# Roots on GpSimd instead of a Newton chain, and a later turn of the normalised row, in a sequence of 48 rows

## The reference

```python
def l2norm(t):
    return t / jnp.maximum(jnp.linalg.norm(t, axis=-1, keepdims=True), 1e-12)

def attn_layer(x, Wqkv, qs, ksc, Wo):
    q, k, v = jnp.split(x @ Wqkv, 3, -1)            # heads of 64
    q = l2norm(q) * qs
    k = l2norm(k) * ksc
    q = q * cos * scale + rotate_half(q) * sin * scale
    k = k * cos / scale + rotate_half(k) * sin / scale
    return local_attention(q, k, v) @ Wo

def ffn_layer(x, g, bln, W1, b1, W2, b2):
    mu = x.mean(-1, keepdims=True)
    var = ((x - mu) ** 2).mean(-1, keepdims=True)
    xn = (x - mu) / jnp.sqrt(var + 1e-05) * g + bln
    a, gate = jnp.split(xn @ W1 + b1, 2, -1)
    return a * jax.nn.gelu(gate, approximate=False) @ W2 + b2
```

## Time and profile before

| | |
|---|---|
| median of 3 runs | 6878.74 us (6875.73 to 6879.80) |
| the profiled execution, its own time | 6877.37 us |
| its span, first to last instruction | 6875.6 us |
| granted TensorE clock, mean over the span | 0.915 |
| instructions | 123524 |
| TensorE matmul, weight load | 85%, 62% |
| VectorE, ScalarE, GpSimd | 65%, 63%, 34% |

### The profile page before, as it was taken

How to read it: one execution, slowest core, us unless ns; L and a number is a source line. 1 busy time by engine, 2 the same in 40 slices (tenths; PEclk the granted TensorE clock), 3 DMA queues, 4 the chain that set the end, 5 groups by cost and what they waited for, 6 DMA issues and landing times. The chain is left out here.

```text
span 6875.6 us, 123524 instructions
## 1 busy us (share of the span) xinstructions
PE 5845.8 (85%) x41538; PEld 4263.2 (62%) x41538; DVE 4476.8 (65%) x17416; ACT 4328.3 (63%) x13318; POOL 2327.9 (34%) x1802
## 2 busy tenths in 40 slices
PE   8884888888888888886588888888888888787989
PEld 7773565666666656664366656656666666566778
DVE  4453777777777777774577777777777776444432
ACT  5511677777777777772377777777777776444643
POOL 0000544444444444440354444444444442000000
PEclk9995999999999999996699999999999999888999
DMA  0000000000000000000000000000000000000000
GB/s 10 19 1 5 16 6 9 5 10 8 11 8 1 14 5 10 8 1 3 19 1 11 8 9 8 3 10 8 10 8 1 13 5 1 5 1 3 1 25 7
DMA packets 30976, 53.56 MB, mean 8 GB/s; under 512 B 7688, under 2 KB 17168, under 8 KB 29712
## 3 DMA queue, kind: packets, MB, share of 16 engines
q1 hardware_dynamic: 30352, 45.66, 2.1%
HBM read 44.60 MB, written 1.05 MB: 7 GB/s over the span
## 5 line engine op out<-in xcount | busy, mean ns | idle before, releaser
L1539 PE MATMUL bank<-wA,next_rowT 128*128 128x512 f32 x2304 | 1290.2, 687 | 217.2 <-DVE turnB L1868 139.7
L1701 POOL TENSOR_TENSOR turnA<-raw,ropes 128x512 f32<-128x512 f32 x768 | 967.1, 1269 | 1453.8 <-ACT raw L1748 1425.1
L1724 ACT ACTIVATE pairs<-pairs,negmax 128x128 f32<-128x128 f32 (+1 forms) x3072 | 1239.6, 419 | 19.5 <-DVE negmax L1829 16.1
L1829 DVE CUSTOM_DVE_ANT_0 pairs<-bank,bands,big 128x128 f32<-128x128 f32 (+1 forms) x3072 | 941.4, 362 | 233.6 <-PE bank L1468 230.2
L1708 POOL TENSOR_TENSOR qk<-turnA,turnB 128x512 f32<-128x512 f32 x768 | 968.6, 1272 | 20.9 <-DVE turnB L1868 20.9
L1539 PEld LDWEIGHTS bank<-wA,next_rowT 128*128 128x128 f32 x2304 | 427.0, 208 | 656.3 <-issue 316.9
L1714 POOL TENSOR_TENSOR qk<-qk,big 128x1024 f32<-128x1024 f32 x192 | 366.1, 1907 | 1100.2 <-DVE recip L1950 1100.2
L251 POOL TENSOR_TENSOR rstd<-vareps,neg_half 128x2 f32<-128x2 f32 x56 | 39.0, 697 | 1802.9 <-DVE vareps L240 1802.9
L1724 ACT ACTIVATION_READ_ACCUMULATOR pairs<-pairs,negmax 128x1 f32 x3072 | 628.5, 205 | 0.0
L1731 ACT ACTIVATE pairsT<-bank 128x512 f32<-128x512 f32 x768 | 468.9, 611 | 204.7 <-PE bank L1481 204.6
L1868 DVE TENSOR_TENSOR turnB<-bank,ropes 128x512 f32<-128x512 f32 x768 | 522.6, 680 | 0.5 <-issue 0.5
...
## 6 DMA issues: line engine op xcount, KB each, us to landing
...
```

What stands on the lines that cost most here:

```text
L1539: pe.matmul(side_bank(i)[:, :], c.next_rowT[:, t * P:(t + 1) * P], wqkv[:, k * 512:(k + 1) * 512], start=True, stop=True).then_inc(s.chunk ...
L1701: g.tensor_tensor(c.turnA[:, m % 2, :].rearrange("p (h d) -> p h d", h=8), c.raw[:, m % 4, :].rearrange("p (h d) -> p h d", h=8), cos, ALU ...
L1724: last = a.activation(tile, tile, ACT.Exp, scale=-1.0, bias=c.negmax[:, 2 * p + side, t:t + 1], accum_out=c.pair_sums[:, p % 4, t, side:si ...
L1829: last = v.tensor_tensor_reduce(c.pairs[:, 2 * (p % 4) + side, AT[t]:AT[t] + SPAN[t]], c.bank[side][:, AT[t]:AT[t] + SPAN[t]], c.bands[:, ...
```

## The change

1. VectorE's Newton chains are gone. What is left of them on VectorE is a guard (maximum with 1e-24) on the 32 columns of a group, as a two-tensor instruction with a constant column, at the end of slots 2 and 5 instead of 3 and 6, and the variance plus epsilon, likewise with two tensors.
2. GpSimd takes the roots by its power: "root0" in slot 3 ahead of "add3", "root1" in slot 6 ahead of "add7", 32 columns each, and a third one of 2 columns for the variances, behind "scale0".
3. The normalisation moves from VectorE's slot 3 to the end of its slot 4, and becomes scalar_tensor_tensor with the root as a second tensor; the statistics stay at the end of slot 3.
4. TensorE transposes xn at the end of slot 5 instead of in slot 4, and multiplies the gates behind slot 6's contexts instead of ahead of them; ScalarE's copy of xn moves to slot 6.
5. In `plain_attention` seven semaphores are shared between its two uses; its instructions stay. `setup` fills two constant columns in place of one.

The core of the diff ("..." stands for what is left out):

```diff
-DVE_RSQRT_SLOTS = {3: 0, 6: 1}
-POOL_SLOTS = {1: ("cos0", "cos1", "add0"), 2: ("cos2", "add1", "cos3", "add2"), 3: ("add3", "scale0"),
-              4: ("cos4", "cos5", "add4"), 5: ("cos6", "add5", "cos7", "add6"), 6: ("add7", "scale1")}
+DVE_GUARD_SLOTS = {2: 0, 5: 1}
+POOL_SLOTS = {1: ("cos0", "cos1", "add0"), 2: ("cos2", "add1", "cos3", "add2"), 3: ("root0", "add3", "scale0"),
+              4: ("cos4", "cos5", "add4"), 5: ("cos6", "add5", "cos7", "add6"), 6: ("root1", "add7", "scale1")}
...
-    ff_var = slice(32, 32 + HALVES)
-    ss = c.big[:, at:at + 68]
+    ss = c.big[:, at:at + 64]
+    ff_var, ff_rstd = c.big[:, at + 64:at + 64 + HALVES], c.big[:, at + 66:at + 66 + HALVES]
...
-                if p == 6 and has_turn(T - 2):
-                    pe_gates(pe, T - 2, (s.qT_copied, (T + 1) * 4 + (1 if following else 0)))
...
-                if p == 4 and has_turn(T - 2):
-                    pe_turn_normed(pe, T - 2)
+                if p == 6 and has_turn(T - 2):
+                    pe_gates(pe, T - 2, (s.qT_copied, (T + 1) * 4 + (1 if following else 0)))
...
+                if p == 5 and has_turn(T - 2):
+                    pe_turn_normed(pe, T - 2)
...
+                elif item[:4] == "root":
+                    g.wait_ge(s.squares_ready, q * 2 + m + 1)
+                    g.tensor_tensor(norms(rs[q % 2], m), norms(ss, m), c.neg_half[:, 0:32], ALU.pow).then_inc(s.rs_ready, 1)
...
+        def pool_ff_root(g, f):
+            g.wait_ge(s.var_ready, f + 1)
+            g.tensor_tensor(ff_rstd, ff_var, c.neg_half[:, 0:HALVES], ALU.pow).then_inc(s.rstd_ready, 1)
...
+                if p == 6 and has_turn(T - 2):
+                    act_normedT(a, T - 2)
...
-        def dve_roots(v, x, y):
-            n = x.shape[-1]
-            ints, a, b, y2 = c.ints[:, 0:n], c.newton[:, 0, 0:n], c.newton[:, 1, 0:n], c.newton[:, 2, 0:n]
-            step.after(v.tensor_scalar(x, x, 1e-24, None, ALU.max), v)
-            step.after(v.tensor_scalar(ints, x.bitcast(I32), 1, None, ALU.logical_shift_right), v)
-            step.after(v.tensor_scalar(a.bitcast(I32), ints, -1.0, MAGIC, ALU.mult, ALU.add), v)
-            for src, dst in ((a, b), (b, a), (a, y)):
-                step.after(v.tensor_tensor(y2, src, src, ALU.mult), v)
-                step.after(v.scalar_tensor_tensor(out=y2, in0=y2, scalar=-0.5, in1=x, op0=ALU.mult, op1=ALU.mult), v)
-                step.after(v.scalar_tensor_tensor(out=dst, in0=y2, scalar=1.5, in1=src, op0=ALU.add, op1=ALU.mult), v)
...
-            step.after(v.tensor_scalar(ss[:, ff_var], ff_mv[:, :, 1], LN_EPS, None, ALU.add), v)
-
-        def dve_ff_normalise(v, f, rstd):
+            v.tensor_tensor(ff_var, ff_mv[:, :, 1], c.guards[:, 1:2].broadcast_to((P, HALVES)), ALU.add).then_inc(s.var_ready, 1)
+
+        def dve_ff_normalise(v, f):
+            v.wait_ge(s.rstd_ready, f + 1)
             for t, n, src in ff_halves(f):
-                last = v.tensor_scalar(c.xn[:, t, n * (D // 2):(n + 1) * (D // 2)], src, ff_mv[:, t, 0:1],
-                                       rstd[:, t:t + 1], ALU.subtract, ALU.mult)
+                last = v.scalar_tensor_tensor(out=c.xn[:, t, n * (D // 2):(n + 1) * (D // 2)], in0=src,
+                                              scalar=ff_mv[:, t, 0:1], in1=ff_rstd[:, t:t + 1].broadcast_to((P, D // 2)),
+                                              op0=ALU.subtract, op1=ALU.mult)
             last.then_inc(s.normed, 1)
...
-        def dve_prepare(v, q, slot, f=None):
-            if slot in DVE_RSQRT_SLOTS:
-                g = DVE_RSQRT_SLOTS[slot]
+        def dve_prepare(v, q, slot):
+            if slot in DVE_GUARD_SLOTS:
+                g = DVE_GUARD_SLOTS[slot]
 
                 v.wait_ge(s.chunk_rotated, q * ROTATED + 4 * g + 4)
-                if f is None:
-                    dve_roots(v, norms(ss, g), norms(rs[q % 2], g))
-                else:
-                    dve_ff_stats(v, f)
-                    dve_roots(v, ss[:, 0:32 + HALVES], rs[q % 2][:, 0:32 + HALVES])
-                v.memset(c.recip[:, 0, 31:32], 0.0).then_inc(s.rs_ready, 1)
-                if f is not None:
-                    dve_ff_normalise(v, f, rs[q % 2][:, ff_var])
+                v.tensor_tensor(norms(ss, g), norms(ss, g), c.guards[:, 0:1].broadcast_to((P, 32)), ALU.max).then_inc(s.squares_ready, 1)
...
-                ff = T - 2 if p == 3 and has_turn(T - 2) else None
                 if following:
-                    dve_prepare(v, T + 1, p, ff)
-                elif ff is not None:
-                    dve_ff_alone(v, ff)
+                    dve_prepare(v, T + 1, p)
+                if p == 3 and has_turn(T - 2):
+                    dve_ff_stats(v, T - 2)
+                if p == 4 and has_turn(T - 2):
+                    dve_ff_normalise(v, T - 2)
...
+                        if slot == 3 and has_turn(q - 3):
+                            pool_ff_root(g, q - 3)
+                for f in range(T1 - 3, T1):
+                    pool_ff_root(g, f)
```

More of the change, by code:

```diff
@@ L111, in allocate @@
     c.V = sb("V", [P, HALVES, NH, DH])
-    c.one = sb("one", [P, 1])
+    c.guards = sb("guards", [P, 2])
     c.sums = sb("sums", [P, HALVES, NH])
@@ L175, in _ @@
             for tile, value in ((c.ident, 0.0), (c.identb, 0.0), (c.causal, 0.0), (c.bands, 0.0),
-                                (c.shift, 0.0), (c.carry, 0.0), (c.one, 1.0), (c.neg_half, -0.5)):
+                                (c.shift, 0.0), (c.carry, 0.0), (c.neg_half, -0.5), (c.guards[:, 0:1], 1e-24),
+                                (c.guards[:, 1:2], LN_EPS)):
                 last = v.memset(tile[:, :], value)
@@ L578, in scalar @@
         a.activation(c.ctxT[:, 1, :], c.bank[5][:, 0:S], ACT.Identity).then_inc(self.sharesT_ready, 1)
+PLAIN_STEPS = LN_STEPS + 3 * (B - 1) + 1
 def plain_attention(nc, sem, c, name, io, x, causal, affine):
@@ L590, in plain_attention @@
     core = NarrowHeads(c, causal)
-    loaded, bias_scaled = sem(name + "_weights"), sem(name + "_bias_scaled")
-    proj_in_psum, step_v = sem(name + "_proj_in_psum"), sem(name + "_steps")
-    v_in_psum, v_ready = sem(name + "_v_in_psum"), sem(name + "_v_ready")
-    out_in_psum = sem(name + "_out_in_psum")
+    (loaded, bias_scaled, proj_in_psum, step_v, v_in_psum, v_ready, out_in_psum), before = c.shared.take(
+        "plain", ("weights", "bias_scaled", "proj_in_psum", "steps", "v_in_psum", "v_ready", "out_in_psum"), B)
+    nth = before // B
+    steps_before = nth * PLAIN_STEPS
     wq, wk = c.wA[:, 0:D], c.wA[:, D:2 * D]
@@ L607, in _ @@
                 n += 16
-            sp.wait_ge(loaded, n)
+            sp.wait_ge(loaded, nth * 112 + n)
         @block.tensor
         def _(pe):
-            pe.wait_ge(loaded, 112)
+            pe.wait_ge(loaded, nth * 112 + 112)
             norm.transpose(pe, 0)
@@ L622, in one_row @@
                 last.then_inc(v_in_psum, 1)
-                pe.wait_ge(v_ready, b + 1)
+                pe.wait_ge(v_ready, before + b + 1)
                 core.tensor(pe, b, lambda: final or norm.transpose(pe, b + 1))
@@ L640, in _ @@
         def _(a):
-            a.wait_ge(loaded, 112)
+            a.wait_ge(loaded, nth * 112 + 112)
             a.mul(c.cols[:, 16:17], c.cols[:, 0:1], scale).then_inc(bias_scaled, 1)
-            a.wait_ge(bias_scaled, 1)
+            a.wait_ge(bias_scaled, nth + 1)
             a.activation(c.cols[:, 30:31], c.cols[:, 0:1], ACT.Exp)
@@ L647, in one_row @@
             def one_row(b, final):
-                a.wait_ge(proj_in_psum, b * 2 + 1)
+                a.wait_ge(proj_in_psum, (before + b) * 2 + 1)
                 a.activation(c.qT[:, 0, :], c.bank[0][:, 0:S], ACT.Identity, scale=scale, bias=c.cols[:, 16:17])
-                a.wait_ge(proj_in_psum, b * 2 + 2)
+                a.wait_ge(proj_in_psum, (before + b) * 2 + 2)
                 a.activation(c.kT[:, 0, :], c.bank[1][:, 0:S], ACT.Identity, bias=c.cols[:, 1:2]).then_inc(core.qk_ready, 1)
@@ L660, in _ @@
             core.clear_values(v)
-            v.wait_ge(loaded, 112)
-            norm.vector(v, 0, Steps(v, step_v, 0, LN_STEPS))
+            v.wait_ge(loaded, nth * 112 + 112)
+            norm.vector(v, 0, Steps(v, step_v, 0, LN_STEPS, steps_before))
             def one_row(b, final):
-                step = Steps(v, step_v, b, 3, LN_STEPS)
-                v.wait_ge(v_in_psum, b + 1)
+                step = Steps(v, step_v, b, 3, LN_STEPS + steps_before)
+                v.wait_ge(v_in_psum, before + b + 1)
                 for t in range(HALVES):
@@ L672, in one_row @@
                 core.vector(v, b, lambda: final or norm.vector(v, b + 1, step))
-                v.wait_ge(out_in_psum, b + 1)
+                v.wait_ge(out_in_psum, before + b + 1)
                 add_rows(v, step, x, b, c.bank[7][:, 0:S], c.rows[:, 1, :])
@@ L1393, in windowed_transformers @@
      s.rowT_in_psum, s.xT_ready, s.chunk_in_psum, s.chunk_copied, s.chunk_squared,
[L1394 removed]
```

(7 more changed lines are left out.)

8 lines of the change are left out of this document (2 added, 6 removed).

## The result

| | before | changed |
|---|---|---|
| median of 4 runs | 6877.75 us (6875.73 to 6879.80) | 6635.44 us (6629.29 to 6636.48) |
| profiled span | 6875.6 us | 6633.7 us |
| granted clock, mean | 0.915 | 0.936 |
| busy PE, DVE, ACT, POOL | 85%, 65%, 63%, 34% | 86%, 63%, 65%, 52% |

The ratio is 0.9643, with a 95% interval of 0.9631 to 0.9655: the changed kernel is faster by 242 us, where 167 were forecast.

The account below looks back on a forecast made before the run. No engine is full; hand-overs bound it, chiefly TensorE's wait for the normalised row behind VectorE. Saving 2.8 less 0.9 for the clock, 1.9 us over 90 turns (171), plus 3 for edges: 6711 us; range 6570 to 6870.

Parts of the forecast that it names:

- rival 1: Whole kernel: as worked, with the number of dips and the waits at the boundary open, 6625 to 6790 us; chance 0.55.
- rival 3: Small gain: every turn dips and VectorE loses a whole instruction at each boundary, 6795 to 6860 us; chance 0.14.
- rival 4: Slower: TensorE's wait moves to slot 5, so the low clock falls wholly on work, 6900 to 6965 us; chance 0.13.
- Rival 5: No effect: GpSimd's queue becomes the bound, TensorE waiting for group 1's scaled keys, 6865 to 6890 us; chance 0.06.
- rival 2: VectorE waits less: cheap 32-column root, perhaps normalisation meeting no running GpSimd instruction, 6430 to 6590 us; chance 0.12.
- The root of 32 columns: GpSimd's power on 32 columns takes 5.41 us, from the slope through its 2- and 16-column times; bounds 2.90 and 11.2.
- The variance's sum waits for root 0: VectorE's two-tensor sum, ready before slot 4, waits for GpSimd's running root; slot 4 still starts 4.03 us earlier.
- The normalisation: End of VectorE's slot 4: kept halves wait for GpSimd's cos4 and cos5, so slot 5 starts only 1.65 us earlier.
- TensorE: It waits 2.3 us in slot 5; slots 4 and 5 end 2.8 us a turn sooner at full clock.
- The clock: TensorE's low clock after its wait: half of the turns have a dip costing 1.8 us, 0.9 on average.
- The remaining 34.9 us are TensorE's own and stay: The turn outside slots 4 and 5 is TensorE's own work and keeps its length of 34.9 us.
- The edges: Prologue +7.4 us a stack (+15) for two roots in a row; tails -6 and turns without normalisation -6; sum +3.

Follow-up runs that it names:

- run 5: The changed kernel with two more VectorE instructions (maximum of two SBUF operands, 128x64) behind the variance's sum, under root 0: 6644.94 us.
- run 4: The changed kernel with the variance's root moved ahead on GpSimd, right behind root 0, before sum 3 and the scaling of the keys: 6541.73 us.
- run 7: The changed kernel with the variance's root right behind root 0 on GpSimd and the whole row put into PSUM: 6298.61 us.
- Run 8: The changed kernel with root 1 taken twice on GpSimd, once into a scratch: 6673.47 us.
- run 1: The kernel before with the later normalisation, turn of the row and gates alone, both Newton chains kept on VectorE: 6677.18 us.
- run 2: The changed kernel with the row's turn and gates back in their old places and the variance's root right behind root 0: 6652.11 us.
- run 9: The kernel before, order and Newton chains as they were, with the whole row in PSUM: 6688.76 us.
- run 10: The kernel before with the later turn of the row, Newton chains kept on VectorE, and the whole row in PSUM: 6608.51 us.
- run 3: The changed kernel with the normalisation written as before, with two scalars instead of a broadcast second tensor: 6680.06 us.
- run 12: The changed kernel with root 0 taken twice on GpSimd, once into a scratch: 7202.38 us.

## Why the prediction was right, and where its steps were off

**Time and rival.** 6711 was forecast, 6635 measured, near the lower end of rival 1 (6625 to 6790). Rivals 3, 4 and 5 didn't happen, nor did 2 as a whole. What rival 4 feared did happen in small: the one wait in slot 5 is followed by a low clock that falls on work (see the clock).

**The root of 32 columns:** 5.41 us from the slope of the earlier trace rows, 5.44 measured. Of the two rows and the rate of an add (rival 2), the rows were right: GpSimd's sum takes 1.27 us for 512 columns, its power 5.44 for 32.

**The variance's sum waits for root 0:** wrong. It takes 0.16 us under the root (run 5 shows that width isn't the reason). VectorE so starts slot 4 0.45 us before TensorE's slot 4 (1850.92 against 1851.37), where I had 0.97 after it. Rival 2 had this as one of its two parts, for another reason.

**The normalisation:** it ends and slot 5 starts 7.55 us after TensorE's slot 4 start; I had 7.67. That is two errors which cancel: VectorE is there 1.4 us sooner, but stands 0.77 us for the variance's root, which I had ready in time because I had VectorE late; run 4 prices this wait. The two kept halves wait for L1705 as worked, though they last 1.23 us each in the mean, where I had 0.9.

**TensorE:** I had 0.7 us of waiting in slot 4 and 2.3 in slot 5; it is none and 3.25. Slots 4 and 5 last 14.42 us in the mean, and my 13.57 plus 0.9 for the clock is 14.47.

**The clock:** I took half of the turns with a dip that costs 1.8 us. In the steady part 78 of 90 have one, in the turn above 3.41 us at 0.51, all worked. What they cost is seen from slot 5's first chunk to slot 6: 4.70 us in the mean, against 3.76 in run 7, which has no low clock in its turns. That is 0.94 us a turn, so the term of 0.9 was met, but by luck: the dips are nearly twice as frequent and cost some 1.1 us each. The total low-clock time fell from 754 to 471 us, since before two waits in a row were followed by 6.14 us at 0.51.

**"The remaining 34.9 us are TensorE's own and stay":** this step failed. Slot 6 fell from 8.37 to 7.92 us. In front of its scores TensorE stood 0.39 us for no partner; this is the kernel before, with the gates L1602 behind:

```profile
2022.09 0.77 PE L1468 MATMUL bank<-kT,qT 64*128 64x128 f32 x8 [0.39 <-issue]
2022.79 1.99 PE L1602 MATMUL bank<-xT,wC 128*128 128x256 f32 x8
```

In the changed kernel the scores follow at once:

```profile
1866.56 0.77 PE L1472 MATMUL bank<-kT,qT 64*128 64x128 f32 x8
1867.25 0.66 PE L1496 MATMUL bank<-ident,recip 128*64 128x128 f32 x8
```

Slot 6 is 8.36 or 8.37 in all four kernels with the old places and 7.91 to 7.95 in all others, whoever takes the roots. Over 90 turns this is 41 us. What in the old sequence makes the engine stand there was not tried.

**The edges:** the prologue was forecast at +7.4 us a stack. From a stack's first transpose to its first attention add it is 117.8 us against 121.0. The second Newton chain stood in front of the copies of kT, which I didn't see: these start at 712.63 where they started at 718.14, and the first transpose of probabilities comes 6.5 us earlier. The root's lateness came as forecast, but later and smaller, as VectorE's wait at the keys of group 1:

```profile
712.63 0.69 DVE L1867 COPY kT<-bank 128x512 f32<-128x512 f32 x1 [2.47 <-PE bank L1566]
...
728.93 0.69 DVE L1867 COPY kT<-bank 128x512 f32<-128x512 f32 x1 [7.98 <-PE bank L1566]
```

So the prologue is -3.2 a stack. From the last attention add to the end of a stack it is 24.4 and 23.2 us against 28.5 twice, -9.4.

**The sum,** in the profiled executions: 47 turns of each stack fell by 225.0 us together (4698.7 to 4473.7), the starts by 6.4, the ends by 9.4: 240.8 of the 241.9 us. I had 168. The 73 that I lacked are 41 in slot 6, 21 in the prologue, 3 in the tails, and some 8 in the turns.

**Rival 5:** I had TensorE want the scaled keys of group 1 in slot 7, with 3.4 us to spare. Run 8 makes them 5.4 us later and no steady turn is longer. The transposes of slot 7 are those of the second pair; group 1's are turned in slots 0 and 3 of the next turn (PE_LATE_QKT_SLOTS). A low chance, but from a misread table.

**What remains open:** why the power leaves VectorE alone, and what makes the gap of 0.39 us. Of the clock the traces show the place and leave the length open: where TensorE waits in slot 4 (before, runs 1, 2, 9, 10) none of the low clock of slots 4 and 5 lies behind the start of slot 5's chunks; where it waits in slot 5 alone (changed, runs 3, 4, 5, 8, 12) 2.8 to 3.9 us a turn do. Why a mean wait of 2.04 us in slot 5 of run 4 draws as much of it as one of 3.41 in the changed kernel isn't shown.
